# Key and query projections as three fp32r products, with normalisation and splitting on GpSimd

## The reference

```
h = group_norm(x, gamma, beta)                 # per image
q, k, v = wq h + bq, wk h + bk, wv h + bv      # 128 x 128 times 128 x 1024
w = softmax(q^T k * 128**-0.5)                 # 1024 x 1024
out = x + wp (v w^T) + bp
```

## Time and profile before

| | |
|---|---|
| median of 3 runs | 2206.46 us (2204.09 to 2207.37) |
| the profiled execution | 2202.45 us |
| its span, first to last instruction | 2200.7 us |
| PE busy in the span | 2103.0 us (96%) |
| DVE | 1810.8 us (82%) |
| ACT | 1713.7 us (78%) |
| POOL | 521.2 us (24%) |

### The profile page before, as it was taken

How to read it: one execution, slowest core, us unless ns; L and a number is a source line. 1 busy time by engine, 2 the same in 40 slices (tenths; PEclk the granted TensorE clock), 3 DMA queues, 4 the chain that set the end, 5 groups by cost and what they waited for, 6 DMA issues and landing times. The chain is left out here.

```text
span 2200.7 us, 59773 instructions
## 1 busy us (share of the span) xinstructions
PE 2103.0 (96%) x24652; PEld 1090.8 (50%) x24652; DVE 1810.8 (82%) x3176; ACT 1713.7 (78%) x3107; POOL 521.2 (24%) x689
## 2 busy tenths in 40 slices
PE   2999999999999999999999999999979999999998
PEld 0244444434344443444444344444438888888887
DVE  2888889888898988889898988989837777777776
ACT  1378787787878778787777878777778888888887
POOL 3113030312303031230303123030023333333331
PEclk9999999999999999999999999999999999999999
DMA  6053334526243351633335263443111111112111
GB/s 75 13 80 54 64 60 64 80 56 92 49 69 61 61 80 52 96 53 65 63 67 83 49 90 53 65 64 64 35 55 49 56 60 44 64 39 69 46 44 51
DMA packets 81747, 133.95 MB, mean 61 GB/s; under 512 B 17632, under 2 KB 50528, under 8 KB 81504
## 3 DMA queue, kind: packets, MB, share of 16 engines
q1 hardware_dynamic: 78240, 129.70, 32.8%
q10 hardware_dynamic: 3264, 0.79, 0.2%
HBM read 53.12 MB, written 17.83 MB: 32 GB/s over the span
## 5 line engine op out<-in xcount | busy, mean ns | idle before, releaser
L449 DVE TENSOR_REDUCE h_half_nmax<-h_s_ps 128x1 f32<-128x512 f32 x2048 | 1281.8, 684 | 176.8 <-PE h_s_ps L683 155.5
L600 ACT ACTIVATE h_probs<-h_st_ps 128x512 f32<-128x512 f32 x2048 | 1099.9, 601 | 306.1 <-PE h_st_ps L683 293.6
L683 PE MATMUL h_s_ps<-h_krep,h_qrep 96*32 96x512 bf16 x8192 | 822.7, 386 | 44.1 <-SPq L234 29.2
L683 PE MATMUL h_st_ps<-h_qrep,h_krep 99*32 99x512 bf16 x8192 | 810.5, 381 | 15.0 <-ACT h_probs L600 10.7
L674 PE MATMUL h_pv<-h_probs,h_vT 128*32 128x512 f32 x4096 | 534.9, 594 | 2.5 <-issue 1.5
L683 PEld LDWEIGHTS h_s_ps<-h_krep,h_qrep 96*32 96x32 bf16 x8192 | 227.5, 96 | 441.1 <-DVE h_half_nmax L449 211.1
L683 PEld LDWEIGHTS h_st_ps<-h_qrep,h_krep 99*32 99x32 bf16 x8192 | 229.4, 97 | 344.0 <-ACT h_probs L600 152.5
L1339 PE MATMUL o_s<-o_k,o_q 128*128 128x512 f32 x768 | 224.4, 428 | 8.1 <-DVE o_q L1160 5.8
L349 POOL TENSOR_SCALAR h_nparts<-h_nmax 128x16 bf16<-128x16 f32 x64 | 16.3, 255 | 896.4 <-DVE h_nmax L457 896.4
L1339 PE MATMUL o_pv<-o_pT,o_vT 128*128 128x512 f32 x768 | 208.1, 406 | 0.8 <-ACTq L1266 0.8
L1154 DVE TENSOR_TENSOR o_pT<-o_t,o_pT 128x512 fp32r<-128x512 f32 x256 | 164.5, 684 | 44.1 <-ACT o_pT L1291 41.6
(11 more groups left out here) (116 smaller groups left out, 1316.7 us busy)
## 6 DMA issues: line engine op xcount, KB each, us to landing
h_krep<-h_kp SPq DMA_DIRECT2D x96, 256.0 KB, 8.9
h_qrep<-h_qp SPq DMA_DIRECT2D x192, 128.0 KB, 6.5
x_res<-out_dram SPq DMA_DIRECT2D x24, 512.0 KB, 3.8
num<-av SPq DMA_DIRECT2D x128, 64.0 KB
rrep<-rden_dram SPq DMA_DIRECT2D x16, 512.0 KB
out_dram<-o_y SPq DMA_DIRECT2D x16, 512.0 KB
out_dram<-h_y SPq DMA_DIRECT2D x15, 512.0 KB, 2.6
o_x_in<-out_dram SPq DMA_DIRECT2D x15, 512.0 KB, 3.5
```

The source lines that it names most:

```text
L449: reduce = nc.vector.tensor_reduce(half_nmax[:, c, unit:unit + 1], s_ps[bank(2 * n + c)][:, :], AX.X, ALU.max, negate=True)
L600: nc.scalar.activation(probs[g % 2][:, j, :], st_ps[bank(n)][:, :], ACT.Exp, scale=1.0 / CH ** 0.5).then_inc(exp_done, 1)
L683: product = nc.tensor.matmul(to[columns, :], stationary[:, columns], moving, start=True, stop=True)
```

## The change

In `one_head`, the projections of keys and queries are made by `split_product` from parts of `h` and of the weights. Value projections stay fp32 and read `h` as before. POOL takes over the normalisation from ACT and makes the parts: `split_weights` for the 256 weight columns of queries and keys, `normalise_and_split` for the two halves of the input. The three places k0, k1 and q0 move one tile later. PE waits at the averages for `w_ready` (POOL passes on the arrival of the weights) instead of the DMA, and before k0 and k1 for the parts of their half.

```diff
-    PLACES = {"avg": (0, 1), "k0": (1, 2), "k1": (2, 2), "q0": (3, 2), "v0": (5, 1),
+    PLACES = {"avg": (0, 1), "k0": (2, 2), "k1": (3, 2), "q0": (4, 2), "v0": (5, 1),
               "q1": (6, 2), "v1": (7, 1)}
...
+        h_parts = sb("h_parts", [P, 2, T], F32R)
+        w_parts = sb("w_parts", [P, 2, 2 * P], F32R)
...
+            def split_weights(par):
+                pool.wait_ge(w_dma[par], 16)
+                pool.sem_inc(w_dma[par], -16)
+                pool.sem_inc(w_ready, 1)
+                weights = wg[par][:, 0:2 * P]
+                own.done(nc.gpsimd.tensor_copy(w_parts[:, HI, :], weights))
+                own.done(nc.gpsimd.tensor_tensor(w_parts[:, LO, :], weights, w_parts[:, HI, :].bitcast(F32), ALU.subtract))
+
+            def normalise_and_split():
+                for c in range(2):
+                    cols = slice(c * HALF, (c + 1) * HALF)
+                    own.done(nc.gpsimd.tensor_scalar(h[:, cols], x_in[:, cols], co[:, 2:3], co[:, 3:4], ALU.mult, ALU.add))
+                    if c == 1:
+                        pool.sem_inc(x_used, 1)
+                    split(h[:, cols], h_parts[:, HI, cols], h_parts[:, LO, cols], h_parts_ready)
+
             def stage_g(u, par, finish=False):
+                split_weights(par)
                 coefficients(u + 1, par)
+                normalise_and_split()
                 if finish:
...
-                    if tile == PLACES["avg"][0] and not (last and u == 1):
-                        act.wait_ge(scale_ready, u + 1)
-                        normalised()
...
-            def project(par, c, column):
-                nc.tensor.matmul(misc[:, :], wg[par][:, column:column + P], h[:, c * HALF:(c + 1) * HALF],
-                                 start=True, stop=True).then_inc(misc_for_act, 1)
+            def project(c, column):
+                cols = slice(c * HALF, (c + 1) * HALF)
+                split_product(misc[:, :], lambda part: w_parts[:, part, column:column + P],
+                              lambda part: h_parts[:, part, cols]).then_inc(misc_for_act, 1)
...
-                            pe.wait_ge(w_dma[1 - u], 16)
+                            pe.wait_ge(w_ready, u + 1)
...
-                            if name == "k0":
-                                pe.wait_ge(h_ready, u + 1)
-                            project(1 - u, int(name[1]), W_K if name[0] == "k" else W_Q)
+                            if name in ("k0", "k1"):
+                                pe.wait_ge(h_parts_ready, 2 * u + int(name[1]) + 1)
+                            project(int(name[1]), W_K if name[0] == "k" else W_Q)
```

More of the change, by code:

```diff
@@ L963, in one_head @@
         coef_ready = sem("coef_ready")
-        scale_ready = sem("scale_ready")
-        h_ready = sem("h_ready")
+        h_parts_ready = sem("h_parts_ready")
         x_dma = sem("x_dma")
@@ L969, in one_head @@
         x_used = sem("x_used")
+        w_ready = sem("w_ready")
         w_used = sem("w_used")
@@ L1034, in coefficients @@
                 own.done(tt(co[:, 5:6], gs[:, 0:1], co[:, 2:3], ALU.mult))
-                tt(co[:, 3:4], wg[par][:, W_BETA:W_BETA + 1], co[:, 5:6], ALU.subtract).then_inc(scale_ready, 1)
+                own.done(tt(co[:, 3:4], wg[par][:, W_BETA:W_BETA + 1], co[:, 5:6], ALU.subtract))
             def split(source, hi, lo, ready):
@@ L1230, in _ @@
             own = Own(act, act_own)
[L1232 to L1242, removed]
             def evacuate(n, name, c, par):
@@ L1301, in body @@
                     act.sem_inc(rinv_ready, -BODY)
-                    act.sem_inc(scale_ready, -2)
                 act.sem_inc(misc_for_act, -taken["act"])
@@ L1428, in body @@
                     pe.sem_inc(stats_ready, -2)
-                    pe.sem_inc(h_ready, -2)
-                    pe.sem_inc(w_dma[0], -16)
-                    pe.sem_inc(w_dma[1], -16)
+                    pe.sem_inc(h_parts_ready, -4)
+                    pe.sem_inc(w_ready, -2)
             body(first=True)
```

## The result

Before 2204.09 us (median of 5 runs, 2201.41 to 2207.37), after 2193.07 (5 runs, 2192.76 to 2194.24): ratio 0.9949 [0.9935, 0.9964], faster by about 11 us. The direction holds, and so does the main mechanism (PE's own matmuls bound the units). The base and two sizes do not, and the argument on ACT holds only for the old order of the places. One later run of the changed kernel, 2415.78 us, was in a slow state and is left out of its median.

The account below looks back on a forecast made before the run. PE was taken to bound the single-head half; 14 x 0.66 = 9.2, plus 0.2, less 0.8 in the first unit, gives 8.6 us off 2206.46, so 2197.9 us, range 2194 to 2204.5.

Parts of the forecast that it names:

- The direction: Whole kernel: the changed kernel is faster, chance 0.81, against 0.13 for the same and 0.06 for slower.
- The base: Starting time of the absolute forecast: 2206.46 us, the median of three runs, from which the saving was taken.
- the argument on ACT: Single-head units: normalising ACTIVATEs of 1.52 us and a 0.75 wait leave ACT, not the bound; nothing comes off the end.
- PE bounds the units: Single-head half: PE is busy 420.44 of 420.44 us, so a microsecond off PE is one off the end.
- 0.165 per projection: Key and query projections on PE: three fp32r products take 0.695 us for 0.86, saving 0.66 per unit.
- Weight loads hidden: Projections on PE: each 188 ns weight load is covered by a 232 ns matmul and costs nothing; uncovered 0.19 each.
- POOL's 6.1 us: POOL per unit: weight parts, normalisations, casts and subtractions add 6.1 us beside 12.5 of 35; POOL stays far from bounding.
- w_ready early: PE's wait at the averages: POOL's increment doesn't wait for its subtraction, so is about 1 us early; cost 0.
- q0's slack: First query projection, now after tile 4: its parts are ready 1.0 us before the scores needing them; cost 0.
- Rival 2: Wait for q0's parts before tile 6's scores: 0.85 us stall per unit, 3.5 us slower, 2210.0; chance 0.04.
- The first unit loses 0.8: First single-head unit: q0 waits behind o1 in the shared bank, tile 5 starts at 1658.5 for 1657.73, 0.8 us lost.
- best bound: Low end of the forecast case's own range, 2195.2 us, from 9.8 us saved over projections plus 1.5.

Follow-up runs that it names:

- experiment 2: Changed kernel with single fp32 matmuls for the key and query projections and no parts made; unit 35.04 us, median 2203.78 us, ratio to before 0.9993.
- experiment 5: Changed kernel with a fourth product (low part by low part) in each key and query projection; unit 35.29 us, median 2208.06 us, ratio to before 1.0018.
- experiment 9: Changed kernel with one of the four projections (k0) as an fp32 matmul; unit 34.47 us, one run of 2197.56 us.
- experiment 10: Changed kernel with three of the four projections (k0, k1 and q0) as fp32 matmuls; unit 34.80 us, one run of 2202.87 us.
- experiment 1: Changed kernel with ACT normalising as before, POOL still making the parts; unit 34.90 us, median 2205.3 us, ratio to before 0.9996.
- experiment 7: Changed kernel with q0 one more tile later, at tile 5; unit 40.92 us, one run of 2295.05 us.

## Why the prediction missed

- **PE bounds the units, and a microsecond off PE is a microsecond off the end.** Right. PE never waits in a steady unit of the changed kernel; experiments 2, 5, 9 and 10 follow the number and kind of matmuls to within 0.07 us of a unit.
- **0.165 per projection.** Right for each of three (0.163). The saving per unit was taken as 0.66 and is 0.73. This is a mis-sized term, 14 x 0.07 = 1.0 us. It lies in the groups of scores and products between the projections (3.62 for 3.65 in a tile without one), which the sum left as they were; its cause is open.
- **Weight loads hidden.** Right: three loads of 0.19 in a projection of 0.69. The Trainium skill (TensorE: Matmul & The Clock Gate, The mechanism) says in one line that a load overlaps only from another row group, and this 0.69 doesn't agree with it. The same section also lets a load go ahead into a background weight buffer, and with that the 0.69 does agree.
- **ACT: nothing comes off the end.** True against the old unit, wrong for the changed kernel, though the sum was the same either way. Without the relief, experiment 1 loses 9.5 of the 10.2 us. I had argued with ACT's margin in the old order, where k0 stood between the normalisation and the scores that need the division, and had moved k0 away in the same change.
- **POOL's 6.1 us.** Measured 0.39 + 0.73 + 2 x (0.77 + 0.61 + 1.30) = 6.5; the normalisation took 0.77 for 0.65 estimated, within its bounds. It hides behind PE. (The load of x_in, released at 1785.1, would land at 1788.6 and not 1789.0, which changes nothing.)
- **w_ready early.** Right. Its price if late was too low: 0.99 a unit instead of 0.32.
- **q0's slack.** In the changed kernel q0's parts are there 1.4 us before the scores of tile 6 (POOL's subtraction ends at 1799.21, the scores start at 1800.62 in the timeline), for 1.0 worked out: safe. Rival 2 priced lateness at its length; with a wait of 3 us experiment 7 shows twice that, for the clock falls.
- **The first unit loses 0.8.** The mechanism was right (q0 behind DVE's reading of o1). Against the start of the part, tile 5 starts 0.3 later than before (1658.86 - 1622.54 for 1657.73 - 1621.75). I had let DVE come half of 1.3 us earlier; it came 1.2 earlier (1657.09 for 1657.54, with a start 0.8 later). To the averages the unit loses 0.1, where the sum had 0.6: 0.5 us. attn ends at 1649.50, 26.96 after the start of the part for 26.55 worked out. PE waits 1.63 for it, which I had not named; even so o0 stands 1.2 earlier than before, so this costs nothing against the old kernel.
- **The base.** This is the step that put the time outside the range: "the median of the three runs is 2206.46 ... and I predict against it: 2197.9". Five runs of the same kernel have the median 2204.09, and they spread by some 6 us; the two profiles of it, 3.4 us apart in span, differ only ahead of the single-head part. Of the 4.8 us between 2197.9 and 2193.07, 2.4 are this base and 1.6 the sizes (10.2 found for 8.6, of which the two terms above explain 1.5); 0.8 stay in the spread. The low end of the range, 2194.0, was the best bound (2195.2) with only 1.2 for the spread of the runs. With 2204.09 as the base the same sum gives 2195.5 and the same best bound 2192.8, below the measured time; with 10.2 for 8.6 but the old base it gives 2196.3, inside the range. So the base alone put the time outside.

## What to carry to other kernels

When a change moves work out of a stretch of the bound engine, work out the margins of the others again in that stretch: an engine whose relief was worthless in the old order may decide whether the saving arrives. Price a wait of PE by more than its length: here a quarter of a microsecond for a short one and, at 3 us, as much again for the clock. Take the base of an absolute forecast from as many runs as there are, and widen the range by their spread. And compare runs by the part of the trace that was changed: it repeated here to 0.1 us, where whole times spread by 4 to 6.

## What the runs showed of the hardware

- An fp32 matmul of 128x512 takes 0.86 us on the chain, three fp32r ones 0.69, four 0.93.
- After a wait of 0.2 to 0.3 us, with the granted clock at 1.00, the next group of matmuls takes 0.24 to 0.30 longer on the chain (0.93 for 0.69, 1.67 for 1.37). 0.16 of it is the overlap with the group before, which a wait ends.
- Groups of six products of 128x512 with nothing else changed come in two lengths, 1.37 or 1.39 for scores (kernel after and kernel 5); the cause is open.
- After a wait of 3.0 us in every unit the granted clock was 0.56 on average over 6.5 us and back at 1.00 in the stretch after them.
- A semaphore increment on POOL passed beside its running instruction (recorded at 1707.5, the subtraction ending at 1708.78). With a wait for the subtraction ahead of it, POOL idled 1.05 us at the loop's end and 0.36 in mid-body before its next instruction.
